# Two attention passes of one block: third transfer buffers, a later fetch, and normalisation and rounding on ScalarE instead of VectorE

## The reference

```python
attn_in = _adaln(x, cond, ln1_w, ln1_b, g1_w, g1_b, b1_w, b1_b)
x = _attn(attn_in, attn_in, sa_wq, sa_wkv, sa_wo, sa_bo) + x
cross_in = _adaln(x, cond, ln1_w, ln1_b, g1_w, g1_b, b1_w, b1_b)
ctx_n = _ln(context, ca_lnc_w, ca_lnc_b)
x = _attn(cross_in, ctx_n, ca_wq, ca_wkv, ca_wo, ca_bo) + x
ffn_in = _adaln(x, cond, ln2_w, ln2_b, g2_w, g2_b, b2_w, b2_b)
```

## Time and profile before

| what | value |
|---|---|
| median of 3 runs (lowest to highest) | 4076.74 us (4074.68 to 4083.11) |
| the profiled execution: time, span | 4081.0 us, 4079.2 us |
| busy share of the span: PE, DVE, POOL, ACT | 94%, 77%, 70%, 60% |
| mean granted clock of PE | 0.992 of full speed |

### The profile page before, as it was taken

How to read it: one execution, slowest core, us unless ns; L and a number is a source line. 1 busy time by engine, 2 the same in 40 slices (tenths; PEclk the granted TensorE clock), 3 DMA queues, 4 the chain that set the end, 5 groups by cost and what they waited for, 6 DMA issues and landing times.

```text
span 4079.2 us, 92937 instructions
## 1 busy us (share of the span) xinstructions
PE 3852.5 (94%) x32822; PEld 3294.9 (81%) x32822; DVE 3158.6 (77%) x6610; ACT 2465.3 (60%) x10244; POOL 2864.6 (70%) x2674
## 2 busy tenths in 40 slices
PE   7999999999989999999999999899999999999999
PEld 6777777777779997888888888777777877778998
DVE  7888889999875557878878787888888888875443
ACT  6999998888963344555555555555555555554333
POOL 5777777777767776666666666677676777766776
PEclk9999999999999999999999999999999999999999
DMA  2101111111111123676766667666666676773110
GB/s 81 31 29 33 33 46 48 48 39 42 53 60 42 45 81 125 206 221 200 223 207 215 209 206 232 208 208 217 207 220 215 211 223 208 223 226 96 49 45 32
DMA packets 415216, 544.98 MB, mean 134 GB/s; under 512 B 58524, under 2 KB 311968, under 8 KB 414752
## 3 DMA queue, kind: packets, MB, share of 16 engines
q1 hardware_dynamic: 414684, 539.03, 41.9%
q10 hardware_dynamic: 68, 0.02, 0.0%
HBM read 220.11 MB, written 184.55 MB: 99 GB/s over the span
## 4 chain that ended last, share of the span: by engine, by line
PE 45%; DVE 14%; POOL 11%; issue 9%; DMA 9%; ACT 8%; SPq 4%; ACTq 0%; POOLq 0%; DVEq 0%
PE BANKS L628 11%; PE BANKS L629 10%; PE BANKS L630 10%; ACT PR L926 5%; DMA p_scratch<-TR 5%; POOL PR L1265 4%; PE BANKS L708 3%; PE BANKS L823 3%; DMA PB<-p_scratch 2%; POOL KT L1284 2%; PE BANKS L787 2%; PE BANKS L775 2%; SPq L601 2%; POOL QT L1284 2%; DVE SN L1146 2%
## 5 line engine op out<-in xcount | busy, mean ns | idle before, releaser
L1265 POOL TENSOR_TENSOR PR<-PR,RL 128x512 f32<-128x512 f32 x1024 | 1065.7, 1044 | 523.4 <-DVE RL L1078 522.2
L942 ACT ACTIVATE PR<-BANKS,NM 128x128 f32<-128x128 f32 x2048 | 719.4, 377 | 541.7 <-DVE NM L1132 541.7
L926 ACT ACTIVATE PR<-BANKS,NM 128x128 f32<-128x128 f32 x2048 | 728.6, 414 | 12.7 <-DVE NM L1065 10.5
L628 PE MATMUL BANKS<-HH,WH 128*128 128x512 f32 x1632 | 681.6, 418 | 2.1 <-ACT HF L969 1.6
L629 PE MATMUL BANKS<-HL,WH 128*128 128x512 f32 x1632 | 642.6, 394 | 0.0
L630 PE MATMUL BANKS<-HH,WL 128*128 128x512 f32 x1632 | 641.7, 393 | 0.0
L926 ACT ACTIVATION_READ_ACCUMULATOR PR<-BANKS,NM 128x1 f32 x2048 | 521.2, 255 | 0.0
L1146 DVE TENSOR_TENSOR SN<-BANKS,ROPE 128x512 f32<-128x512 f32 x512 | 348.4, 681 | 129.5 <-DMA SW<-SN 128.8
L942 ACT ACTIVATION_READ_ACCUMULATOR PR<-BANKS,NM 128x1 f32 x2048 | 443.1, 216 | 0.0
L1085 DVE STREAM_TRANSPOSE TR<-PR 128x512 f32<-128x512 f32 x512 | 351.6, 687 | 101.9 <-DMA p_scratch<-TR 56.7
L628 PE MATMUL BANKS<-WH,OH 128*128 128x256 f32 x1280 | 378.8, 296 | 37.1 <-DVE OL L1150 31.8
(11 more groups left out here) (134 smaller groups left out, 10667.3 us busy)
## 6 DMA issues: line engine op xcount, KB each, us to landing
SW<-SN SPq DMA_DIRECT2D x1024, 128.0 KB, 2.7
p_scratch<-TR SPq DMA_DIRECT2D x256, 512.0 KB, 3.4
PB<-p_scratch SPq DMA_DIRECT2D x1024, 128.0 KB, 3.1
x_scratch<-X SPq DMA_DIRECT2D x80, 512.0 KB, 3.3
X<-x_scratch SPq DMA_DIRECT2D x80, 512.0 KB, 4.2
CX<-in_ctx SPq DMA_DIRECT2D x32, 384.0 KB, 4.2
X<-in_x SPq DMA_DIRECT2D x16, 512.0 KB, 4.0
out<-X SPq DMA_DIRECT2D x16, 512.0 KB, 2.9
```

Of the source, the lines that this page charges most:

```text
L628: e.matmul(o, lh, rh, start=first and i == 0, stop=False)
L926: made = e.activation(pr[:, r], bank[:, r], ACT.Exp, bias=nm[:, h:h + 1], accum_out=RL[npr(t)[0]][:, h:h + 1])
L942: made = e.activation(pr[:, r], bank[:, r], ACT.Exp, bias=nm[:, h:h + 1], accum_out=RL[npr(t)[0]][:, h:h + 1])
L1265: e.tensor_tensor(p3, p3, RL[npr(t)[0]][:, :].unsqueeze(2).broadcast_to([128, 4, 128]), ALU.mult).then_inc(s_nrm, 1)
```

## The change

1. SW and TR get a third buffer, with a constant NSW for SW. SP's swap r now waits for POOL's addition r-2 no longer, but for r-3; DVE's transposition waits for the store of three units before.
2. The get moves from T+5 to T+6, so on SP it stands behind the put of the next unit.
3. In passes 3 and 4 Z, the context's normalisation, HH and the context's merge are made by ACT. ACT computes scale x input + bias, so POOL makes RM = -(mean x root) with two more operations (CRM for the context), and ACT's normalisation waits for them.
4. In pass 5 DVE waits for ACT's last Z and HH in turn. The shared region of SBUF grows by 1024 elements a partition, and the DMA scratch of the program is set from 2048 to 256.

The diff, cut to its core (the rest are buffers, semaphores and the removal of the same stages from the vector program):

```diff
-NP1, NTR, NPT1, NSC = 4, 2, 3, 4
+NP1, NTR, NSW, NPT1, NSC = 4, 3, 3, 3, 4
...
-                    for stage, lag in (("q1", -5), ("q1_add", -3), ("k1", -4), ("k1_add", -2), ("scores", 0), ("max", 0), ("put", 4), ("get", 5),
+                    for stage, lag in (("q1", -5), ("q1_add", -3), ("k1", -4), ("k1_add", -2), ("scores", 0), ("max", 0), ("put", 4), ("get", 6),
...
                         q.wait_ge(s_rt, r + 1)
-                        q.wait_ge(s_zz, r - 1)
+                        q.wait_ge(s_zz, r - NSW + 1)
                         for i in range(2):
-                            e.dma_start(SW[r % 2][i:128:2, :], SN[r % 2][1 - i:128:2, :]).then_inc(s_sw[r % 2], 16)
+                            e.dma_start(SW[r % NSW][i:128:2, :], SN[r % 2][1 - i:128:2, :]).then_inc(s_sw[r % NSW], 16)
...
+                for p, g in at["c_merge", tick]:
+                    if p == 1:
+                        continue
+                    u, k = h_of(p, g, True)
+                    q.wait_ge(s_hl, 2 * u + 2)
+                    q.wait_ge(s_hm, cq(p, g))
+                    e.activation(HH[k][64:128, 1, :], HL[k][64:128, 1, :].bitcast(F), ACT.Copy).then_inc(s_hm, 1)
+
+                for stage, context in (("split", False), ("c_split", True)):
+                    for x in at[stage, tick]:
+                        if KIND[x.p] != "b":
+                            continue
+                        u, k = h_of(x.p, x.g, context)
+                        q.wait_ge(s_hf, hfs["c_turn" if context else "turn", x] + 1)
+                        q.wait_ge(*hid.free((context, x.p, x.g)))
+                        q.wait_ge(s_hh, 2 * u + x.c)
+                        e.activation(HH[k][:, x.c, :], HF[u % 2][:, x.c, :], ACT.Copy).then_inc(s_hh, 1)
+
+                for x in at["norm", tick]:
+                    if KIND[x.p] != "b":
+                        continue
+                    u = xq(x.p, x.g)
+                    pp, gg = divmod(u - 1, NG)
+                    q.wait_ge(s_rm, 2 * ((x.p - 3) * NG + x.g) + 2)
+                    q.wait_ge(s_turn, hparts["turn", Part(pp, gg, 1, 0)] + 1)
+                    q.wait_ge(s_z, u)
+                    made = e.activation(Z[:, x.b, :], X[u % NX][:, x.b, :], ACT.Identity, bias=RM[u % 2][:, x.b:x.b + 1], scale=RS[u % 2][:, x.b:x.b + 1])
...
+                    q.wait_ge(s_crm, 2 * x.g + 2)
+                    made = e.activation(CX[:, x.b, :], CX[:, x.b, :], ACT.Identity, bias=CRM[:, x.b:x.b + 1], scale=CRS[:, x.b:x.b + 1])
...
+                    if KIND[p] == "b":
+                        q.wait_ge(s_rs, u + 1)
+                        e.tensor_tensor(RM[u % 2][:, :], MV[u % 2][:, :, 0], RS[u % 2][:, :], ALU.mult).then_inc(s_rm, 1)
+                        q.wait_ge(s_rm, 2 * ((p - 3) * NG + g) + 1)
+                        e.tensor_tensor(RM[u % 2][:, :], RM[u % 2][:, :], NEG[:, :], ALU.mult).then_inc(s_rm, 1)
```

More of the change, by code:

```diff
@@ L265, in build @@
         RS = [sb(f"RS{i}", [128, G]) for i in range(2)]
-        CST, CMV, CVE, CRS = (sb(k, s) for k, s in (("CST", [128, G, 6]), ("CMV", [128, G, 2]), ("CVE", [128, G]), ("CRS", [128, G])))
+        RM = [sb(f"RM{i}", [128, G]) for i in range(2)]
+        CST, CMV, CVE, CRS, CRM = (sb(k, s) for k, s in (("CST", [128, G, 6]), ("CMV", [128, G, 2]), ("CVE", [128, G]), ("CRS", [128, G]), ("CRM", [128, G])))
         MODS = sb("MODS", [128, 5, 2, NB])
@@ L283, in build @@
             sb("PR_L1", [128, 512 * NP1], stack=spare)
-            SW = [sb("SW0", [128, 512], stack=spare)]
+            SW = [sb(f"SW{i}", [128, 512], stack=spare) for i in range(NSW)]
             TR = [sb(f"TR{i}", [128, 1024], stack=spare) for i in range(NTR)]
-            SW += [sb("SW1", [128, 512], stack=spare)]
-        sb("SHARED", [128, 512 * (NP0 + NPT0)])
+        sb("SHARED", [128, 512 * (NP1 + NSW + 2 * NTR)])
         CX = sb("CX", [128, G, 256])
@@ L354, in build @@
         s_qk, s_rt, s_zz, s_v1, s_va = (sem(k) for k in ("qk", "rt", "zz", "v1", "va"))
-        s_sw = [sem(f"sw{i}") for i in range(2)]
+        s_sw = [sem(f"sw{i}") for i in range(NSW)]
         s_tr = sem("tr")
@@ L978, in _ @@
                     e.activation(o, i, ACT.Identity, bias=CCOL[:, 2 + x.c:3 + x.c], scale=CCOL[:, x.c:x.c + 1]).then_inc(s_hf, 1)
+                for p, g in at["c_merge", tick]:
[23 more added lines that the diff above has]
+                    made = e.activation(Z[:, x.b, :], X[u % NX][:, x.b, :], ACT.Identity, bias=RM[u % 2][:, x.b:x.b + 1], scale=RS[u % 2][:, x.b:x.b + 1])
+                    if x.b == G - 1:
+                        made.then_inc(s_z, 1)
+                for x in at["c_norm", tick]:
+                    q.wait_ge(s_crm, 2 * x.g + 2)
+                    made = e.activation(CX[:, x.b, :], CX[:, x.b, :], ACT.Identity, bias=CRM[:, x.b:x.b + 1], scale=CRS[:, x.b:x.b + 1])
+                    if x.b == G - 1:
+                        made.then_inc(s_cz, 1)
                 for p, g, j in at["up", tick]:
@@ L1169, in _ @@
                 for x in at["norm", tick]:
-                    if x.p < 2 and xq(x.p, x.g) > 1:
+                    if KIND[x.p] == "b" or (x.p < 2 and xq(x.p, x.g) > 1):
                         continue
@@ L1200, in _ @@
                     e.bn_aggr(CMV[:, x.b, :], CST[:, x.b, :]).then_inc(s_cmv, 1)
[L1202 to L1208, removed]
                 for p, g in at["c_root", tick]:
@@ L1222, in _ @@
                         e.tensor_tensor(HL[k][:, x.c, :], bank[:, :], HH[k][:, x.c, :].bitcast(F), ALU.subtract).then_inc(s_hlc, 1)
+                for p, g in at["c_merge", tick]:
+                    if p == 4:
                         continue
[L1224 to L1228, removed]
                     u, k = h_of(p, g, True)
-                    q.wait_ge(s_hlc if p == 1 else s_hl, 2 * u + 2)
+                    q.wait_ge(s_hlc, 2 * u + 2)
                     rounded(HH[k][64:128, 1, :], HL[k][64:128, 1, :].bitcast(F), p).then_inc(s_hm, 1)
```

24 lines of the change are left out of this document (18 added, 6 removed).

## The result

| | before | changed |
|---|---|---|
| median (lowest to highest), us | 4079.31 (4074.68 to 4083.11) | 4188.81 (4184.05 to 4195.25) |
| the profiled execution: time, span | 4081.0, 4079.2 | 4195.25, 4193.4 |
| busy: PE, DVE, POOL, ACT | 94%, 77%, 70%, 60% | 93%, 72%, 68%, 63% |
| mean granted clock of PE | 0.992 | 0.980 |

The changed kernel takes 1.027 times as long, with a 95% interval of 1.025 to 1.029: 110 us more, where the prediction had 56 us less. The time is outside its range of 3978 to 4088, above its upper end. It lies next to rival B (4172), and B's mechanism, a fetch behind a store and too late, is what came, though not in every unit.

A forecast was written before the change was run, and what follows sets the result against it. PE's in-order work was taken as the bound. Savings of 49 us in pass 4 and 7 in pass 3, together 56, took 4081.0 to 4025, and 4.3 for the median gave 4021 us; range 3978 to 4088.

The forecast's parts named there:

- rival B: Passes 3 and 4: the fetch behind the store is late in every unit, 8.55 us a unit, 4172 us; chance 0.18.
- The later fetch: SP's queue, passes 3 and 4: the fetch, issued nearly a unit later, just fits, by 0.4 to 1.2 us.
- tipping point: Fetch in passes 3 and 4: a landing 6.2 us after a start at P + 10.2, where rival B begins.
- units with other transfers: Fetches near X or context transfers: 0.8 us for each of two units per pass 4 group, 0.20 per unit; pass 3 0.10.
- DVE is relieved: DVE in pass 4: 7.3 us of 66 per group go, 85% busy to about 74%; PE's OL wait goes, 31 us.
- ACT's new wait: ACT's normalisation waiting for POOL's RM: costed at 0, at most 1 us per root, 48 us.
- something holds DVE in part of its Z: DVE's Z at 0.747 us against CX's 0.434, same shape: a port lock shared with POOL agrees; adds nothing to the sum.
- SP's wait for POOL KT: SP's swaps in pass 4, waiting for POOL's addition two back: 132.5 us in 97 units, to be gone.
- lever of the third SW: SP's queue: a swap waits for the addition three back, so SP reaches the store earlier, 1.4 us each.
- ceiling: PE's stalls in passes 3 and 4: at most 94 us to win, 20 in pass 3 and 74 in pass 4.
- A: Passes 3 and 4: the fetch always fits and everything goes, 94 us, 3983 us; chance 0.14.
- C: Gain given back: fetches land in about 6.2 us or ACT's RM wait costs 48 us; 4069, up to 4085; chance 0.13.

The follow-up runs named there:

- due-later run: The changed kernel, fetch still at T+6 behind the store, with value products, OH, OL and output projection due a unit later: 4011.78 us, 0.983.

## Why the prediction was wrong, point by point

**The step that failed is the landing in "The later fetch".** It said: four issues take 1.94 us, an issue lands in 3.1, so the fetch is there 4.6 us after its start, "just fits, by 0.4 to 1.2 us". For the kernel before that was right: its plain fetches take 4.65 us. But both durations had been read from fetches that waited for their store and so never had one in front. With the store in front issuing the four takes 2.29 us (median of the 91 fetches in pass 4) instead of 1.94, a DMA lands in 3.6 instead of 3.1, and a whole plain fetch takes 5.44 us in pass 3 and 5.56 in pass 4, a quarter of those in pass 3 6.5 or more. That is 0.8 to 0.9 us more than the sum had, against a margin of 0.4 to 1.2. The tipping point of 6.2 us, which the prediction gave for B, lies inside the scatter, and the weight loads wait in about half the units. The scatter itself isn't the store's doing: in the kernel before, over a tenth of all fetches already took 6.2 us or more.

**The second term mis-sized is that of the units with other transfers.** The prediction took 0.8 us for each of two such units per group of pass 4, 0.20 us per unit. The trace has three such units a group (34 in 91), 26 of them waited, and they wait 54.5 us, 1.6 us each or 0.60 over all units. Their fetches take 6.11 us and start at 3.5 us, where the prediction had every start at 1.6 to 2.0; for the median fetch that start was right (1.7 in pass 3, 1.8 in pass 4), for these it was not. The prediction expected X's transfers to do less harm once they no longer stood directly ahead of a fetch; with the fetch first the same units still wait 25.7 us and start at 3.2.

**The weighing of B.** "A store uses DMA time in whole large rows" spoke of throughput. The due-later run shows that throughput was never short, and the time from start to due alone decides. B's unit of 8.55 us was too small for pass 4, 8.79, and too large for pass 3, 8.26. That the kernel came out at 4189 where B had 4172 is luck: B charged 6.9 us to every fetch and nothing to the clock or to the change of passes, and these errors cancel.

**A term that no case had: the clock.** Three short stretches around the longest stall shown above, 3236 to 3248 us (columns as before; the clock is the number behind the busy times), then, from the kernel before, a stretch behind the 2.02 us stall of the earlier trace rows and the score products in it:

```profile
3236.00:3240.00 4.00, 0.82 (x12) 0.62 (x12) 1.12 (x3) 0.60 (x1) 4.00 (x6) 1.00 1.08 269
3240.00:3244.00 4.00, 4.00 (x33) 3.33 (x28) 1.19 (x1) 0.60 (x1) 2.62 (x3) 0.57 0.84 236
3244.00:3248.00 4.00, 4.00 (x23) 3.44 (x22) 3.29 (x10) 3.93 (x19) 0.35 (x1) 1.00 0.16 58
```
```profile
3153.00:3157.00 4.00, 4.00 (x24) 3.29 (x23) 2.13 (x4) 1.69 (x8) 3.03 (x3) 0.57 0.37 116
```
```profile
3152.98 1.62 PE L787 MATMUL BANKS<-KT,QT 64*128 64x128 f32 x16
```

PE stood still for 3.18 us; then the scores took 2.08 us instead of 1.16 at a granted clock of 0.57, which is mostly the lower level, 1.2 GHz, and by 3244 it was back at 2.4 GHz. A stall of 2 us can have the same behind it, as the two rows from the kernel before show; there they were few, and the mean clock of the stretch was 0.99. In the changed kernel it is 0.96: 800 x 0.04 / 0.5 = 64 us at half speed, half of them lost, an estimate of 32 us or 0.35 per unit (28 to 36 us, as 0.96 is rounded). The wait for PB is 70.8 / 91 = 0.78 per unit, and 7.67 + 0.78 + 0.35 = 8.80, against 8.79 measured. PE's busy time says the same in another way: 728.88 / 91 = 8.01 us a unit where it is 785.20 / 103 = 7.62 with the early fetch, at a clock of 1.00. In pass 3, at a clock of 1.00, 7.95 + 42.0 / 109 = 8.34 against 8.26. So the loss in pass 4 is the two together, the waits and what they do to the clock. With the late fetch alone the clock is 0.92.

**What held.** DVE is relieved: 582.82 / 800 = 73% busy in pass 4 (predicted 74%), and the wait for OL has gone. But the size of that term was wrong: I gave it 31 us, and the work on ACT alone brought 18, with OL halved. I had laid the whole of the wait to DVE's load, but with the buffers alone it falls too (24.5 to 18.5), and only with both is it gone. SP no longer waits for its store, DVE's transposition not for the store either. ACT is 161 us busier (2626.2 against 2465.3), where the prediction had about 150. ACT's part, first in pass 4, then its wait in pass 3:

```profile
L997 ACT ACTIVATE HH<-HF 128x512 fp32r<-128x512 f32 x48 | 30.6, 638 | 1.1
...
L1007 ACT ACTIVATE Z<-X,RM,RS 128x256 f32<-128x256 f32 x44 | 27.0, 615 | 1.8 <-POOL RM L1339 0.6
...
L1337 POOL TENSOR_TENSOR RM<-MV,RS 128x4 f32<-128x4 f32 x11 | 2.2, 202 | 0.9
```
```profile
ACT Z L1007 <- POOL RM L1339: 5.1, 12, 0.4
```

RM costs POOL 0.20 us an operation, where I took 0.3 between 0.232 and 1.033, and ACT's new wait is 5.1 us in the whole stretch of pass 3 (0.6 in pass 4), against 0 taken and 48 as the bound. Z takes 0.615 us on ACT where I had the nearest row at 0.403; HH 0.638 against 0.682. All of it is hidden: with the late fetch ACT's part changes nothing. The Trainium skill (ScalarE: Activation LUTs, "Rules for kernel authors") advises VectorE for such arithmetic; the prediction worked out 0.51 us from its budget for Z and 0.72 for HH, where the trace has 0.615 and 0.638. Here ACT was still the better place with two buffers and an early fetch, by 0.4%, and the wait for OL halved with it. On top of the third buffers its gain is not told from none (0.981 against 0.983, intervals that overlap).

The prediction's guess that something holds DVE in part of its Z can be read from the trace before. Of the 113 Z in the two stretches 50 found no instruction of POOL at their start that had over 0.25 us still to run, and took 0.39 to 0.41 us. The other 63 began while POOL was in an addition or multiplication of two tiles, and every one of them ended 0.15 us after POOL's did, after 0.55 to 1.20 us. So an instruction of POOL holds DVE's up for as long as it lasts, and this is the price of the lock that the prediction told of. ACT's 128 Z in the changed kernel show nothing of it: all took 0.60 to 0.65 us.

**SP's wait for POOL KT did not go.** In pass 4 of the changed kernel SP waits as follows:

```profile
SPq L609 <- DVE SN L1183: 184.5, 98, 6.6
SPq L86 <- POOL KT L1318: 73.3, 37, 2.7
SPq L596 <- DVE TR L1122: 24.6, 54, 0.5
```

I had said it gone; 73.3 us are left of 132.5. With the buffers and the early fetch it is 15.8 without ACT's part and 7.5 with it. It goes with the late fetch and does no harm by itself: with the due time a unit later it is 80.3 us, and that kernel has no wait for PB and runs at 0.983. Perhaps SP, which no longer stands in the store's wait, comes to the swaps earlier and waits there; that is argued and not shown.

**The lever of the third SW was mis-sized.** I had seen it ("SP reaches the store earlier", 1.4 us each) and then credited PB's wait with a fall from 0.34 only to 0.20 per unit, since the later fetch used the gain up. Alone it takes the wait for PB away in both passes and brings 67 us of the 94 of the ceiling. The ceiling itself holds: the best kernel is 78 us under before.

The rivals A and C fell with the same runs: A because the fetch doesn't always fit, C because it costs more than the gain and ACT's wait for RM is 5.1 us and not 48.

## What to carry over

A latency read from a trace holds for the neighbourhood it was read in: before a transfer is moved, look at what will stand directly ahead of it on its queue, and take the landing from rows that have such a neighbour, or bound it from the worst of those that have any. Sort the transfers by what goes out ahead of them before taking a median: here little more than a third of the units carried nine tenths of one pass's wait. Where an order has a small margin between a fetch and its use, change the due time first: a unit more of it cost nothing that could be measured and made the whole loss vanish. And try the parts of a change apart: this one held a gain of 1.9% under a loss of 4.6%, one number of one line.

## What the runs showed of the hardware

- A 512 KB store 0.57 us ahead of a fetch of four 128 KB DMAs on one queue raised the landing of each from 3.0 or 3.1 us to 3.6, the issuing of the four from 1.94 to 2.29 us, and the whole fetch, with only swaps besides, from 4.65 to 5.44 and 5.56 us. With the store on ACT's queue 0.55 to 0.8 us ahead the landing was 3.41 (21 fetches), 2.5 to 3.3 us ahead 2.97. With the fetch first it was 3.0, while the store went from 3.3 to 3.7.
- After PE had stood still for 3.18 us its granted clock was 0.57 over the 4 us from 3240, and 16 score products took 2.08 us instead of 1.16. Behind the 2.02 us stall of the earlier trace rows the value products took their usual 1.09, but the clock from 3153 to 3157 was 0.57 too, and the score products took 1.62.
- VectorE's normalisation of 128x256 took 0.39 to 0.41 us, but when POOL was in an instruction on two tiles at its start it ended 0.15 us after POOL's, 63 times of 63.
- An addition or multiplication of 128x4 on POOL took 0.20 us, the power of the same shape 1.02 to 1.03.
- ACT's scale and bias over 128x256 from SBUF took 0.61 us, its read from PSUM of the same shape 0.40.
